# Second attention of a two-layer network: the output projection one slot later, and the residual sum, its statistics, its first scale and its store one slot later

## The reference, cut to what matters

```python
q = _rope(_rms_norm((draft_hidden @ Wq.T).reshape(bsz, draft_len, H, HD), q_norm_w))
k = _rope(_rms_norm((kv_in @ Wk.T).reshape(bsz, total_len, KVH, HD), k_norm_w))
v = (kv_in @ Wv.T).reshape(bsz, total_len, KVH, HD)
scores = jnp.einsum('bhqd,bhkd->bhqk', q, k) * SCALE
probs = jax.nn.softmax(scores, axis=-1)
attn = jnp.einsum('bhqk,bhkd->bhqd', probs, v)
x = x + attn.transpose(0, 2, 1, 3).reshape(bsz, draft_len, H * HD) @ Wo.T
```

## Time and profile before

| | us |
|---|---|
| median of 3 runs | 3103.31 |
| lowest and highest | 3097.90 and 3106.26 |
| the profiled execution | 3106.21 |
| its span | 3104.4 |
| PE busy over the span | 2848.2 (92%) |
| DVE busy over the span | 1829.6 (59%) |
| ACT, POOL busy over the span | 1703.5 (55%), 1741.2 (56%) |

### The profile page before, as it was taken

The page is one execution under the profiler, slowest core; times in us unless marked ns, Lnnn a source line. Parts: engine busy times, 40 slices in busy tenths (PEclk is TensorE's granted clock), DMA queues, the critical chain, the costliest instruction groups (busy, mean ns, idle before and its releaser), DMA issues. The chain is left out here.

```text
span 3104.4 us, 57661 instructions
## 1 busy us (share of the span) xinstructions
PE 2848.2 (92%) x16353; PEld 1637.9 (53%) x16354; DVE 1829.6 (59%) x5590; ACT 1703.5 (55%) x4562; POOL 1741.2 (56%) x2443
## 2 busy tenths in 40 slices
PE   4699999999999969999999999769999999985998
PEld 2366666666666635555555554335444444443665
DVE  4366666666666655444344344458888888863443
ACT  5578777877778732333233223346666666661332
POOL 6467777777777534554444455366666666631222
PEclk9799999999999989999999999889999999997999
DMA  6711121112111153554555456535555545657444
GB/s 241 251 42 56 51 86 48 48 55 79 58 48 55 54 200 120 161 157 125 147 159 151 137 141 186 141 80 113 122 113 123 122 112 122 123 106 286 80 83 70
DMA packets 467529, 360.89 MB, mean 116 GB/s; under 512 B 295520, under 2 KB 366304, under 8 KB 467424
## 3 DMA queue, kind: packets, MB, share of 16 engines
q1 hardware_dynamic: 404912, 282.85, 32.1%
q0 software_dynamic: 16496, 37.79, 6.3%
q10 hardware_dynamic: 46016, 38.99, 4.4%
HBM read 186.23 MB, written 110.39 MB: 96 GB/s over the span
## 5 line engine op out<-in xcount | busy, mean ns | idle before, releaser
L1393 POOL TENSOR_TENSOR e_st<-e_st,e_ws_tile 128x1024 f32<-128x1024 f32 x64 | 123.8, 1935 | 428.1 <-PE e_y L1149 417.2
L752 ACT ACTIVATE a_nrm<-a_mm,a_sc_t 128x128 f32<-128x128 f32 x768 | 290.8, 474 | 123.6 <-POOL a_sc_t L905 123.4
L603 DVE BATCH_NORM_STATS2 a_st<-a_mm 128x6 f32<-128x128 f32 x768 | 170.7, 285 | 289.5 <-PE a_mm L440 206.5
L439 PE MATMUL a_mm<-a_w_hi,a_xq_hi 128*128 128x512 f16 x768 | 296.6, 386 | 22.7 <-POOL a_xq_lo L887 15.7
L1187 ACT ACTIVATE e_hh<-e_ha 128x512 f16<-128x512 f32 x128 | 76.3, 596 | 411.7 <-PE e_ha L1134 410.1
L440 PE MATMUL a_mm<-a_w_hi,a_xq_lo 128*128 128x512 f16 x768 | 296.4, 386 | 0.0
L1282 DVE SCALAR_TENSOR_TENSOR e_hl<-e_ha,e_hh 128x512 f16<-128x512 f32 x128 | 88.4, 691 | 351.6 <-ACT e_hh L1187 351.2
L904 POOL TENSOR_TENSOR a_sc_t<-a_sc_t,a_mhalf 128x4 f32<-128x4 f32 x192 | 203.2, 1058 | 119.0 <-DVE a_sc_t L610 118.7
L1147 PE MATMUL e_y<-e_w2h,e_hh 128*128 128x512 f16 x640 | 242.6, 379 | 0.0
L1148 PE MATMUL e_y<-e_w2l,e_hh 128*128 128x512 f16 x640 | 242.6, 379 | 0.0
L1149 PE MATMUL e_y<-e_w2h,e_hl 128*128 128x512 f16 x640 | 242.6, 379 | 0.0
(11 more groups left out here) (366 smaller groups left out, 8246.6 us busy)
## 6 DMA issues: line engine op xcount, KB each, us to landing
e_st<-in_w SPq DMA_DIRECT2D x128, 512.0 KB, 4.2
disp<-a_empty SPq DMA_DIRECT2D x16, 2084.0 KB
e_st<-in_w1b SPq DMA_DIRECT2D x32, 352.0 KB, 3.1
disp<-a_empty SPq DMA_DIRECT2D x4, 2605.0 KB, 22.8
e_xb<-disp SPq DMA_DIRECT2D x40, 260.5 KB, 4.3
e_xb<-disp ACTq DMA_DIRECT2D x40, 260.5 KB
a_cx<-in_ctxT SPq DMA_DIRECT2D x32, 256.0 KB, 3.3
a_stage<-in_wprojT SPq DMA_DIRECT2D x16, 512.0 KB, 4.7
```

What stands on the lines that cost most here:

```text
L439: pe.matmul(out, xq_hi[:, n, c, :], w_hi[:, t, c, :], start=(c == 0), stop=False)
L752: ins = act.activation(nrm[:, n % 2, i * P:(i + 1) * P], src[:, i * P:(i + 1) * P], ACT.Identity, bias=sc_t[:, n % 2, 3, i:i + 1], scale=s ...
```

## The change

Five offsets in the plans of layer1_attention are raised by one: on PE out_project from 6 to 7, on DVE final and r_stats from 7 to 8, on SP store from 7 to 8, on POOL r_scale from 8 to 9. ACT's plan is the same. No instruction is added or removed, and no wait condition changes. out_project thereby leaves the even slots and stands in the odd ones, behind pv of the next group; final, store and r_stats go from slot 3 to slot 4, r_scale from slot 4 to slot 5.

```diff
-            run_pipeline(sp, [("in", 5, x_turn), ("job", 2, q_turn), ("att", 3, p_turn), ("end", 7, store), ("end", 2, residual), ("in", 1, x_load)],
+            run_pipeline(sp, [("in", 5, x_turn), ("job", 2, q_turn), ("att", 3, p_turn), ("end", 8, store), ("end", 2, residual), ("in", 1, x_load)],
...
-                              ("att", 5, pv), ("att", 6, out_project), ("end", 11, r_transpose), ("end", 13, r_logits),
+                              ("att", 5, pv), ("att", 7, out_project), ("end", 11, r_transpose), ("end", 13, r_logits),
...
-            run_pipeline(dve, [("end", 7, final), ("att", 2, row_scale), ("att", 1, smax), ("job", 2, q_low), ("in", 5, x_low),
+            run_pipeline(dve, [("end", 8, final), ("att", 2, row_scale), ("att", 1, smax), ("job", 2, q_low), ("in", 5, x_low),
...
-                               ("end", 7, r_stats), ("in", 3, x_stats), ("end", 14, r_scores), ("end", 16, r_inverse),
+                               ("end", 8, r_stats), ("in", 3, x_stats), ("end", 14, r_scores), ("end", 16, r_inverse),
...
-            run_pipeline(pool, [("in", 2, c_low), ("job", 0, scales), ("in", 3, x_scale), ("in", 5, tables), ("end", 8, r_scale),
+            run_pipeline(pool, [("in", 2, c_low), ("job", 0, scales), ("in", 3, x_scale), ("in", 5, tables), ("end", 9, r_scale),
```

## The result

| | us |
|---|---|
| the changed kernel, median of 4 runs | 3124.57 (3120.64 to 3128.46) |
| the kernel before on the same chip, median of 4 runs | 3102.64 (3097.90 to 3106.26) |
| ratio | 1.0072, 95% interval 1.0060 to 1.0083 |
| the profiled execution, its span | 3126.64, 3124.8 |

The change costs 22 us, 0.7%. The forecast was 3110, its range ended at 3119. The sum pointed the right way, but at +6.5 us it was a third of what was measured.

A forecast was written before the change was run, and what follows sets the result against it. The prediction took a circle through ACT, DVE, POOL and DMA loads, not PE, to bound the kernel. Terms of +7.9 and -1.4 us made +6.5, taking the median from 3103.3 to about 3110 us; range 3097 to 3119.

The forecast's parts named there:

- The sum: Whole run: +7.9 us for final's new slot and -1.4 us at the end of the stage, +6.5 us together.
- the removed wait: On PE before out_project: its 40.5 us vanish but reappear mainly before the score product; value 0, bounds -40.5 and 0.
- final to slot 4: On DVE between o_low of slot 3 and smax of slot 5: final costs its 0.61 us in 13 batches, +7.9 us.
- r_stats stays in the same stretch: On DVE between o_low of slot 3 and smax of slot 5: r_stats moves from start to end, costing 0.
- r_scale, store, final's cover against out_project: On POOL, SP and DVE: later r_scale and store cost 0; final comes 4.3 us after out_project ends, so no wait.
- The end of the stage: Last batches, after the repeating stretch: 3.5 us gained, 2.1 us lost, sum -1.4 us; bounds -3.5 and +2.1.
- out_project's term: End of the stage, PE: another out_project and the router's product stand before the last out_project; 2.1 us lost.
- final's term of -3.5 us: End of the stage, DVE: batch 14's final, one slot later, no longer waits 2.87 us, so smax comes 3.5 us sooner.
- Rival C: On DVE in final's new stretch: final with its waits costs 0.76 us a period, no end gain, 3113 us; chance 0.25.

The follow-up runs named there:

- the last kernel: e10 with x_stats also moved on VectorE, from behind o_low to ahead of q_low of slot 3: 3077.90 us, ratio 0.9897 to 0.9931.
- e6: e4 with r_stats at offset 9 right ahead of o_low on VectorE, and r_scale at 9: 3092.36 us.
- e10: e6 with out_project back at offset 6: 3090.04 us.
- e1: The kernel before with only out_project moved, from offset 6 to 7: 3119.78 us.
- e2: The changed kernel with out_project back at offset 6, everything else still moved: 3119.78 us.
- e4: The kernel before with out_project at offset 7 and final, still at 7, put right ahead of o_low on VectorE: 3103.07 us.
- e5: e4 with out_project back at offset 6: 3100.38 us.
- e3: The changed kernel with r_stats moved behind r_slots, to the end of VectorE's order within its slot: 3113.08 us.

## Why the prediction was wrong, point by point

- **PE is not the bound; the removed wait is worth 0.** Right. The wait reappeared as said, under the score product and pv (29.4 + 18.3 us, 3.7 a period where 3 were forecast), and two kernels that differ by out_project's place alone have periods of 46.30 and 46.31. By the Trainium skill ("Perfetto Trace Analysis", Identifying the Most-Contended Engine and Optimization Strategy) the gaps of the engine with the highest occupancy were the thing to work on; these traces show nothing gained in the periods by taking away TensorE's regular one. The same section's warning, that for TensorE the share of weight loads is to be read, goes further than the prediction took it: by it TensorE stands at 48% and VectorE, 536.8 of 620 us, at 87%, and VectorE's order is where the 27 us of the last kernel were.
- **final to slot 4, 0.61 us a period.** Right in mechanism and near in size: 0.59 us a period when the cast is taken out of it, 0.68 without the first period. The set-up before it, which the prediction had at 0.15 us and left out of its sum, is in the stretch with 0.18 (0.77 us from o_low to o_low); between 0 and 0.1 us of it reached the period, and the runs don't tell more.
- **"r_stats stays in the same stretch, at its end instead of its start: 0."** This is the step that failed, and it carries the larger part of the miss: 13 casts of 0.66 us too much, 8.6 us. Within the stretch VectorE's sum of work was indeed unchanged, but the order against another engine was not: r_stats went from ahead of the statistics that start POOL's chain to between them and the cast, and the cast ran into POOL's sum. The prediction took each of VectorE's operations at its duration in the trace of before, and never asked what each would stand beside.
- **r_scale, store, final's cover against out_project: 0.** Nothing speaks against it. r_scale stands one slot later in e6 and e10 too, and their periods are explained without it; store was never moved alone. No wait for PE before final in the repeating stretch, with 4.3 us of cover, and e1 shows what it is worth: without it the period is 0.65 us longer.
- **The end of the stage, -3.5 + 2.1 = -1.4.** Wrong: of the 4.9 us measured, one final (it is the thirteenth) and two drawn-out casts make 0.61 + 2 x 0.66 = 1.9, and 3.0 are the end's own. out_project's term was 2.1 us, reckoned at the last group alone; between e2 and the changed kernel it is 4.5, between e4 and e5 6.0, and 8.1 between the kernel before and e1, where final stands close behind it. The prediction missed the out_project of the batch before, which at offset 7 queues behind a pv that waits for its DMA (4.44 us at 2788.04 in the changed kernel), and it took 2.60 us for 12 matmuls, where after that wait a part goes at half the clock: these pv and out_project, 18 matmuls, take 6.3 us (2788.04 to 2794.34), and at the 0.22 us of the full pace some 3.9; the granted clock over 2788 to 2789.5 is 0.50. final's term of -3.5 us did come: in e2, which has it without out_project's, the fifth smax of the end is 2.1 us late (52.0 us behind the thirteenth o_low of slot 3, against 50.0) and the eighth, behind final's old place, 1.4 us early (78.9 against 80.3). But 1.8 us were given back behind it, where ACT's o_high waited 2.30 us for PE, whose out_project ahead of that pv ran for the most part with matmuls 0.43 us apart, at a granted clock of 0.50 (2780.5 to 2785.5). -3.4 + 1.8 + 4.5 = 2.9.
- **The sum.** +7.9 - 1.4 = +6.5 forecast. Found: 7.9 (final) + 8.6 (cast) + 3.0 (end) = 19.5, of 20.1 in the trace. The 0.6 us left went with the cast (8.0 us in e3's periods for 7.3 by its length) and are not explained.
- **Rival C** had the right sign and two small pieces of the cause: the set-up of final's waits is in the stretch, and the gain at the end of the stage did not come. The largest piece, the cast, is not in it, and at 3113 it fell short too.

## What to carry to other kernels

A wait is worth what stands behind it: before removing one, look for the engine that in turn waits for the waiter; if there is none, leave it, as its 40 us are free. In a loop of engines the price list is the stretch without idle: an operation moved out of it, to where the same engine waits anyway, gave 0.78 of its 0.89, 0.76 of 0.83 and, where others then fell beside GpSimd, 0.38 of 0.62 us a period here, and the one moved in cost about its own 0.6. When an operation is moved past another on the same engine, also look at what the ones behind it will then run beside on GpSimd.

## What the runs showed of the hardware

A cast on VectorE of 128 by 2 elements, SBUF to SBUF, takes 0.17 us alone and 0.82 to 0.88 us if it starts during GpSimd's sum of two 128 by 512 float32 tiles: it ends with that sum, within 0.03 us, in 13 of 13 cases. x_low, with two inputs in SBUF, is held too, by 0.3 to 1.0 us (0.95 to 1.70 against 0.68 at the end of the stage), and where it is held by the sum it ends 0.55 us behind it. The holding goes the other way too: where the two start 0.01 us apart (x_low at 2095.83, the sum at 2095.82 in the kernel before), x_low keeps its 0.68 us and the sum takes 1.82 us instead of 1.27. The blocked time stands in the profile as length of the blocked operation, not as idle time before it. smax, which reads PSUM, and r_stats' BATCH_NORM_STATS2, which reads one SBUF tile, kept their 1.22 and 0.69 us beside the same sum. The Trainium skill ("SBUF — State Buffer", Who interferes with whom) says that VectorE and GpSimd share one pair of ports as an exclusive lock, that casts are among the VectorE operations that can ask for it, that tensor_reduce never does on this chip, that a VectorE operation with two SBUF inputs contends with GpSimd's reads, and that the second to issue is blocked until the first ends. The trace agrees for the cast (0.83 us), x_low (1.69 us) and smax (1.22 us). It doesn't show why the cast, 0.17 us long alone, ends only 0.02 us behind the sum.
